# Second attention of a four-layer block: two maxima blocks and the second half of the query transposes move into the next step, the split terms get a second buffer

## The reference, cut to what matters

```python
hn = _layernorm(x, ln1_g, ln1_b)                    # 16 sequences of 256 tokens, 16 heads of width 8
q = (hn @ wq + bq); k = (hn @ wk + bk); v = (hn @ wv + bv)
scores = jnp.einsum('bhqd,bhkd->bhqk', q, k) / jnp.sqrt(jnp.float32(D))
attn = jax.nn.softmax(scores, axis=-1)
o = jnp.einsum('bhqk,bhkd->bhqd', attn, v)
x = x + (o @ wo + bo)
hn2 = _layernorm(x, ln2_g, ln2_b).reshape(-1, h)
logits = hn2 @ gate_w + gate_b
idx = jnp.argmax(logits, axis=-1)                   # one expert for each token
```

## Time and profile before

| | us |
|---|---|
| median of 3 runs | 1882.75 (1875.11 to 1886.69) |
| the profiled execution | 1882.32 |
| its span | 1880.5 |
| PE, DVE, POOL, ACT busy in the span | 1255.7, 1244.0, 1018.8, 727.4 |
| granted PE clock, mean of the span | 0.761 |

### The profile page before, as it was taken

How to read it: one execution, slowest core, us unless ns; L and a number is a source line. 1 busy time by engine, 2 the same in 40 slices (tenths; PEclk the granted TensorE clock), 3 DMA queues, 4 the chain that set the end, 5 groups by cost and what they waited for, 6 DMA issues and landing times.

```text
span 1880.5 us, 28307 instructions
## 1 busy us (share of the span) xinstructions
PE 1255.7 (67%) x8634; PEld 880.8 (47%) x8635; DVE 1244.0 (66%) x2728; ACT 727.4 (39%) x1190; POOL 1018.8 (54%) x1176
## 2 busy tenths in 40 slices
PE   3435333478777777877787779257767776746796
PEld 1223122236666565656665558223433333325685
DVE  6788850177787878787878873167777778743322
ACT  1101001145454454454444553036565555532221
POOL 2356576456666666666666645334445444425554
PEclk7555555578888888888888887669898889878766
DMA  4010004400000000000000000210000000001110
GB/s 132 22 27 15 13 13 81 94 7 1 8 8 8 7 6 6 6 6 6 6 3 3 7 4 6 72 33 12 19 18 16 9 17 17 7 17 44 42 40 12
DMA packets 73354, 40.91 MB, mean 22 GB/s; under 512 B 23811, under 2 KB 68716, under 8 KB 73284
## 3 DMA queue, kind: packets, MB, share of 16 engines
q1 hardware_dynamic: 50530, 24.02, 4.6%
q0 software_dynamic: 20384, 11.67, 3.1%
q10 hardware_dynamic: 2370, 4.35, 0.8%
HBM read 31.11 MB, written 23.87 MB: 29 GB/s over the span
## 4 chain that ended last, share of the span: by engine, by line
PE 33%; DVE 29%; issue 13%; POOL 13%; ACT 7%; DMA 2%; ACTq 1%; POOLq 1%; SPq 0%; DVEq 0%; another core or an unknown queue 0%
PE psum L1138 9%; PE psum L1189 5%; POOL xe_dram L570 4%; DVE terms L1766 4%; DVE o L1606 4%; PE psum L1246 3%; POOL o_inv L618 3%; DVE q_highT L1792 2%; PE psum L1166 2%; POOL got L768 2%; POOL out L777 2%; PE psum L1304 1%; DVE rden L1458 1%; PE psum L1269 1%; DVE silu_g L1700 1%
## 5 line engine op out<-in xcount | busy, mean ns | idle before, releaser
L1138 PE MATMUL psum<-v,attn 128*128 128x64 f32 x2048 | 287.8, 300 | 25.6 <-ACT aggr L870 17.1
L1138 PEld LDWEIGHTS psum<-v,attn 128*128 128x128 f32 x2048 | 271.9, 213 | 61.1 <-issue 44.2
L1766 DVE TENSOR_REDUCE terms<-psum 128x4 bf16<-128x1024 f32 x128 | 156.9, 1226 | 45.5 <-PE psum L1269 43.7
L641 POOL DMA_INDIRECT yg<-ye_dram,routel x128 | 140.1, 1095 | 60.0 <-issue 36.2
L945 ACT ACTIVATE prob<-psum 128x512 f32<-128x512 f32 x256 | 139.5, 602 | 49.7 <-PE psum L1233 45.5
L570 POOL DMA_INDIRECT xe_dram<-rows_out,route x128 | 131.8, 1030 | 39.6 <-issue 39.0
L855 ACT ACTIVATE attn<-psum 128x1024 f32<-128x1024 f32 x128 | 129.9, 1015 | 10.1 <-PE psum L1121 8.9
L1147 PE MATMUL psum<-ident,o 128*128 128x128 f32 x256 | 48.7, 353 | 117.9 <-DVE silu_g L1700 91.0
L618 POOL TENSOR_TENSOR o_inv<-o_max,minus_half 128x16 f32<-128x16 f32 x32 | 107.6, 3364 | 2.7
L658 POOL TENSOR_TENSOR v<-v,inv 128x2048 f32<-128x2048 f32 x16 | 70.7, 4418 | 59.8 <-DVE inv L1586 59.8
L1147 PEld LDWEIGHTS psum<-ident,o 128*128 128x128 f32 x256 | 39.1, 183 | 131.5 <-DVE o L1606 66.5
(11 more groups left out here) (300 smaller groups left out, 3106.5 us busy)
## 6 DMA issues: line engine op xcount, KB each, us to landing
x4n_dram<-x4n SPq DMA_DIRECT2D x16, 256.0 KB, 4.5
w<-in_w POOLq DMA_DIRECT2D x48, 64.0 KB, 2.3
x_in<-in_x SPq DMA_DIRECT2D x8, 256.0 KB, 2.9
xe_dram<-zero_rows SPq DMA_DIRECT2D x8, 256.0 KB, 3.2
x_dram<-x1s SPq DMA_DIRECT2D x8, 256.0 KB, 2.4
xe_dram<-rows_out,route POOLq DMA_INDIRECT x128, 2.1
xe<-xe_dram SPq DMA_DIRECT2D x16, 128.0 KB, 2.4
ye_dram<-ye SPq DMA_DIRECT2D x16, 128.0 KB, 2.2
```

The lines of the kernel that those rows point to most:

```text
L641: pool.indirect_dma_start(yg[fetch.p][:, j, k, :], None, ye_dram, bass.IndirectOffsetOnAxis(ap=where[:, j, K0 + k:K0 + k + 1], axis=0), bo ...
L1138: mm = pe.matmul(psum[:, 4 + j, (head % HALF) * DV:(head % HALF + 1) * DV], attn[g % RING][:, h, c * SEQ + j * P:c * SEQ + (j + 1) * P], v ...
L1766: dve.tensor_reduce(dst[:, :, 2 * m2:2 * m2 + 2], psum[:, 4:6, :].rearrange("q p (b k) -> q p b k", b=2), AX, ALU.max, negate=True).then_i ...
```

## The change

`terms4` becomes two buffers, one for odd and one for even sequences; POOL clears both before the first step, and POOL, ACT and DVE may overwrite one as soon as the sequence two before has been transposed. Maxima blocks 6 and 7 leave part 7 and are done in parts 0 and 1 of the next step, as work of `att`, on PE ahead of that part's scores. Blocks 0 to 5 take parts 3, 4, 5, 6, 7, 7. q4 half 1 goes from part 1 to part 3, q4 half 0 from part 6 to part 7, behind the transposes of `xn4`, which now come ahead of those of `x4n`. The transposes of `o4` use ring[0] where they used ring[1], and ACT copies them out in part 4 behind two more exponentials. On DVE the expert choice comes directly behind the logits, and the residual add with its moments comes ahead of block 1. On POOL the roots of the first normalisation come ahead of the sum that it adds up for the end of the tail.

```diff
-        terms4 = sb("terms4", [P, 2, 2, HEADS, TERMS1, DH], BF16)
+        terms4 = two("terms4", [P, 2, 2, HEADS, TERMS1, DH], BF16)
...
-            pool.memset(terms4[:], 0.0).then_inc(s["set4"], 1)
             for p in range(2):
+                pool.memset(terms4[p][:], 0.0).then_inc(s["set4"], 1)
                 pool.memset(v4[p][:], 0.0).then_inc(s["set4"], 1)
...
             for p in range(2):
+                pool.memset(terms4[p][:, 1, :, :, MAXIMUM, 0:1].rearrange("q j h a -> q (j h) a"), 1.0).then_inc(s["set4"], 1)
                 pool.memset(v4[p][:, :, :, DH:DH + 1], 1.0).then_inc(s["set4"], 1)
...
-                    if not isinstance(front.n, int) or front.n > 1:
-                        hold(s["q4_ps"], 2 * (front.n - 1))
+                    if not isinstance(front.n, int) or front.n > 2:
+                        hold(s["q4_ps"], 2 * (front.n - 2))
...
                 if tail:
                     inverse_deviation("var5", meanvar5, veps5, rstd5, "rstd5", tail.n)
+                if fetch:
...
+                    inverse_deviation("var4", meanvar4, veps4, rstd4_in, "rstd4_in", fetch.n)
...
+                if tail:
                     if not isinstance(tail.k, int) or tail.k > 1:
                         hold(s["x4_stored"][tail.p], 16 * (tail.k - 1))
                     hold(s["plain_made"], tail.n)
                     pool.tensor_tensor(x4n[tail.p][:, :, 0:D], x4[tail.p][:], x3_plain[tail.p][:], ALU.add).then_inc(s["sum_made"], 1)
                 if fetch:
...
-                    if att and g == 1:
+                    if att and g == 3:
                         take_terms(att, "q4", 1, 1)
...
-                    if tail and g == 3:
+                    if tail and g == 4:
                         act.wait_ge(s["o4T_ps"], tail.n)
-                        act.activation(o4T[:], ring[1][:, 0:SEQ], ACT.Copy).then_inc(s["o4T_made"], 1)
+                        act.activation(o4T[:], ring[0][:, 0:SEQ], ACT.Copy).then_inc(s["o4T_made"], 1)
...
-                    if front and g == 6:
+                    if fetch and g == 7:
+                        act.wait_ge(s["x4T_ps"], fetch.n)
+                        act.activation(h4T[:], ring[1][:, 0:SEQ], ACT.Identity, bias=norms[:, 1:2], scale=norms[:, 0:1]).then_inc(s["h4T_made"], 1)
+                    if front and g == 7:
                         take_terms(front, "q4", 0, 1)
                     if tail and g == 7:
                         act.wait_ge(s["x5T_ps"], tail.n)
                         act.activation(h5T[:], ring[0][:, 0:SEQ], ACT.Identity, bias=norms[:, 3:4], scale=norms[:, 2:3]).then_inc(s["h5T_made"], 1)
-                    if fetch and g == 7:
...
-                if front:
+                if att:
+                    readers[1] = [(s["q4_out"], 2 * att.n - 1)]
+                elif front:
                     readers[1] = [(s["h4T_made"], front.n)]
-                elif att:
-                    readers[1] = [(s["q4_out"], 2 * att.n - 1)]
                 elif end:
                     readers[1] = [(s["x4_made"], end.n)]
                 for g in range(PAIRS):
+                    if att and g < 2:
+                        maxima(att, 6 + g)
                     if att:
                         scores4(att, g)
                     if tail and g == 0:
@@ -1302,8 +1306,6 @@
...
-                    if att and g == 1:
-                        turn_terms(att, "q4", 1, 1, [(s["max_made"], PAIRS * att.n), (s["terms4_made"], 6 * att.n)])
                     if end and g == 1:
...
+                    if att and g == 3:
+                        turn_terms(att, "q4", 1, 1, [(s["max_made"], PAIRS * att.n), (s["terms4_made"], 6 * att.n)])
                     if front and g in (3, 4, 5, 6, 7):
-                        maxima(front, (0, 1, 3, 4, 6)[g - 3])
+                        maxima(front, g - 3)
...
                     if tail and g == 3:
-                        b = fill4(1, [(s["o4T_made"], tail.n)], [(s["o4_made"], 2 * tail.n)])
+                        b = fill4(0, [(s["o4T_made"], tail.n)], [(s["o4_made"], 2 * tail.n)])
...
-                    if front and g == 6:
-                        turn_terms(front, "q4", 0, 1, [(s["max_made"], PAIRS * (front.n - 1) + 4), (s["terms4_made"], 6 * front.n)])
                     if att and g == 6:
                         turn_values(att, 0, 0)
+                    if fetch and g == 7:
+                        b = fill4(1, [(s["h4T_made"], fetch.n)], [(s["xn4_made"], fetch.n)])
+                        for j in range(2):
+                            mm = pe.transpose(b[:, j * P:(j + 1) * P], xn4[:, j, :], ident[:])
+                        mm.then_inc(s["x4T_ps"], 1)
+                    if front and g == 7:
+                        turn_terms(front, "q4", 0, 1, [(s["max_made"], PAIRS * (front.n - 1) + 4), (s["terms4_made"], 6 * front.n)])
                     if tail and g == 7:
                         b = fill4(0, [(s["h5T_made"], tail.n)], [(s["x4n_made"], tail.n)])
                         for j in range(2):
                             mm = pe.transpose(b[:, j * P:(j + 1) * P], x4n[tail.p][:, j, D:2 * D], ident[:])
                         mm.then_inc(s["x5T_ps"], 1)
-                    if fetch and g == 7:
-                        b = fill4(1, [], [(s["xn4_made"], fetch.n)])
-                        for j in range(2):
-                            mm = pe.transpose(b[:, j * P:(j + 1) * P], xn4[:, j, :], ident[:])
-                        mm.then_inc(s["x4T_ps"], 1)
-                    if front and g in (4, 6, 7):
-                        maxima(front, {4: 2, 6: 5, 7: 7}[g])
+                    if front and g == 7:
+                        maxima(front, 5)
...
             def half(fetch, front, att, tail, end):
                 for g in range(PAIRS):
+                    if att and g < 2:
+                        take_maxima(att, 6 + g)
                     if front and g == 0:
...
-                    if end and g == 2:
+                    if end and g == 1:
                         for j in range(2):
...
-                    if front and g in (3, 4, 5, 6):
-                        take_maxima(front, (0, 1, 3, 4)[g - 3])
+                    if front and g == 1:
+                        dve.wait_ge(s["high4_made"], front.n)
+                        dve.tensor_tensor(qk4[:], qk4[:], high4[:], ALU.subtract).then_inc(s["rest4_made"], 1)
...
+                    if tail and g == 2:
+                        divide_by_sums(tail, 1, 1)
+                    if front and g == 3:
+                        wait(dve, s["q4_ps"], 2 * (front.n - 2))
+                        take_maxima(front, 0)
                     if end and g == 3:
...
-                    if front and g == 4:
-                        take_maxima(front, 2)
+                    if front and g in (4, 5):
+                        take_maxima(front, g - 3)
                     if fetch and g == 5:
...
                     if front and g == 6:
-                        take_maxima(front, 5)
+                        take_maxima(front, 3)
                     if fetch and g == 7:
...
                     if front and g == 7:
-                        take_maxima(front, 6)
-                        take_maxima(front, 7)
+                        take_maxima(front, 4)
```

More of the change, by code:

```diff
@@ L730, in half @@
                     inverse_deviation("var5", meanvar5, veps5, rstd5, "rstd5", tail.n)
-                    if not isinstance(tail.k, int) or tail.k > 1:
-                        hold(s["x4_stored"][tail.p], 16 * (tail.k - 1))
-                    hold(s["plain_made"], tail.n)
-                    pool.tensor_tensor(x4n[tail.p][:, :, 0:D], x4[tail.p][:], x3_plain[tail.p][:], ALU.add).then_inc(s["sum_made"], 1)
                 if fetch:
@@ L748, in half @@
                     pool.tensor_tensor(rstd4[:], rstd4_norm[:], rstd4_in[:], ALU.mult).then_inc(s["rstd4"], 1)
+                if tail:
+                    if not isinstance(tail.k, int) or tail.k > 1:
+                        hold(s["x4_stored"][tail.p], 16 * (tail.k - 1))
+                    hold(s["plain_made"], tail.n)
+                    pool.tensor_tensor(x4n[tail.p][:, :, 0:D], x4[tail.p][:], x3_plain[tail.p][:], ALU.add).then_inc(s["sum_made"], 1)
+                if fetch:
                     chain.step(pool.tensor_scalar(x3n[fetch.p][:, 0, :], x3l[fetch.p][:, 0, :], meanvar4[:, 0, 0:1], rstd4_in[:, 0:1], ALU.subtract, ALU.mult))
@@ L986, in half @@
                         act.activation(h5T[:], ring[0][:, 0:SEQ], ACT.Identity, bias=norms[:, 3:4], scale=norms[:, 2:3]).then_inc(s["h5T_made"], 1)
-                    if fetch and g == 7:
-                        act.wait_ge(s["x4T_ps"], fetch.n)
-                        act.activation(h4T[:], ring[1][:, 0:SEQ], ACT.Identity, bias=norms[:, 1:2], scale=norms[:, 0:1]).then_inc(s["h4T_made"], 1)
             pipeline(act, half, 5)
@@ L1278, in turn_terms @@
                         at = (2 * a4 + j) * P
```

(2 more changed lines are left out.)

39 lines of the change are left out of this document (17 added, 22 removed).

## The result

| | before | after |
|---|---|---|
| median | 1883.11 us (4 runs, 1875.11 to 1886.69) | 2081.06 us (4 runs, 2063.16 to 2087.19) |
| ratio | | 1.104, 95% interval 1.097 to 1.111 |
| profiled execution's span | 1880.5 | 2061.2 |
| a step, mean of steps 5 to 14 | 26.99 | 39.72 |
| granted clock of PE in these steps | 0.87 | 0.65 |

The change costs 198 us; the forecast said 96, and 2081 lies over its range. The profiled execution is the fastest of the four (2063.16, granted clock 0.718 over the span; the others 0.703 to 0.707 at 2081 to 2087).

A forecast was written before the change was run, and what follows sets the result against it. No engine fills a step; in-order engines wait for each other in one closed chain of sections A, B, C. 82 us for 12 steps, 11 for others, 3.5 for a memset: 96 on 1882.3 gives 1978 us, range 1918 to 2010.

The forecast's parts named there:

- The clock of PE: PE's granted clock in the changed stage: the sum leaves it at 0.87 although a step grows to 33.8 us.
- the sum: A, B and C together: 6.8 us a full step, 82 for 12 steps; with other steps and memset 96 us.
- a rival with 11 in 100: Second rival: PE's clock falls from 0.87 to 0.72, 2.2 us more a step, 2004 us; 11 in 100.
- A: Step's border, from `xn4`'s end to DVE's first bias add: grows 3.2 us, qkv behind two maxima rounds on PE.
- B: From first bias add to block 0's reduce end: grows 1.3 us, mostly block 0 waiting behind q4 half 1.
- C: From block 0's reduce to `xn4`'s end: grows 2.3 us despite two rounds fewer, as y4 and block 1 come late.
- The bank of `picked_b`: In C: `o4` transposes wait for ring[0], read by `picked_b` after block 0's reduce; they start 0.17 us after that reduce.
- Other steps: Steps 1, 2, 3, 16 and 17, counted alike: together +11 us, of which step 3 +5.9.
- The first rival: Moved blocks fill DVE's idle time and ring waits do not bind: -2.2 us a step, 1856 us; 6 in 100.
- the third: A grows as worked out, but `o4T` is early enough that C keeps its two rounds: 1883 us; 9 in 100.
- the fourth: A binds, q4 half 1 finds its bank free, late y4 just eats the two rounds: 1932 us; 17 in 100.

The follow-up runs named there:

- w2: Changed kernel plus 32 PE products a step that nothing reads, ahead of eight PE waits, 12 of them ahead of q4 half 1: 1981.6 us.
- c1: Changed kernel with block 1's reduce ahead of the residual add on DVE again, no added products: 2028.9 us.
- w4: w2 without the 12 added products ahead of q4 half 1, those at the seven other waits kept: 1990.6 us.
- wch: w2 with DVE's expert choice put back behind the division of part 2: 1949.7 us.
- wc: w2 with block 1's reduce ahead of the residual add on DVE: 1962.3 us.
- wbco: wb with block 1 ahead of the residual add, `o4` transposes ahead of the rank products, ACT's copy a part earlier, no added products ahead of y4: 1949.9 us.
- wbest: wch with block 5 directly behind the transposes of `xn4`, block 1 ahead of the residual add, no added products ahead of block 6: 1927.3 us.
- w3: Kernel before the change plus 16 PE products a step that nothing reads, ahead of six PE waits: 1871.6 us, ratio 0.996.
- wb: w2 with q4 half 1 behind block 0, values 0 and the rank products, and 6 added products there instead of 12: 1964.8 us.
- wfull: wbco with block 5 directly behind the transposes of `xn4` and no added products ahead of block 6: 1930.0 us.
- w1: Changed kernel plus three larger products a step that nothing reads, in PE's long pause ahead of q4 half 1: 2057.1 us.
- b1: Changed kernel with q4 half 1 behind block 0, values and rank products on PE, no added products: 2046.8 us.

## Why the prediction was wrong, step by step

**The step that failed** is the one under "The clock of PE": "The changed step leaves PE the same work in 33.8 us", and still the sum kept 0.87. The fall was made a rival with 11 in 100, to 0.72, at 1.5 us for a tenth from two steps, 26 us in all; against it stood "that PE still gets the same bursts". Measured: the same bursts, with longer pauses between them, got 0.65, and from after to w2 39.72 - 33.73 = 6.0 us for 0.28, 2.1 for a tenth (added work in the way would make it look smaller; c1's steps of two lengths give 3.5), 99 us in the whole time. The price was a poor reading too: in the same trace of before, 1567.80:1594.80 takes 27.00 us at 0.94 and 1485.70:1513.80 takes 28.10 at 0.89. In the new order more PE work is on the chain: at the border q4 half 0, the transposes of `x4n` and two blocks stand between the transposes of `xn` and qkv, where one block stood; whether that is why the price is higher was not tested. And waits and clock feed each other, which a fixed fall leaves out: the longer waits of the new order came with a lower clock, and when w2 gave the clock back, DVE's waits for PE shrank with no change to the order (in ten steps, for the maxima blocks from 71.5 us to 46.9, for qkv from 28.6 to 9.7; for y4 hardly, 31.3 to 30.3). What the Trainium skill says (TensorE: Matmul & The Clock Gate, "What's actually happening"), that activity releases the low clock, the runs bear out: added work that nothing reads took 99 us off.

**The order's own cost** was sized nearly right: at w4's 0.88 a step is 34.33, so 7.3 us more than before where the sum had 6.8. That w2 comes within 4 us of 1978 is partly luck: its clock is not the 0.87 of the sum, and B came out 1.5 longer, C 0.8 shorter.

**A** (+3.2): right at the restored clock, 7.45 for 7.21; first in order are the transposes, then two rounds, then qkv, as laid out. In after itself, at half clock, 10.95.

**B** (+1.3): too small, 12.29 for 10.8 in w2. Three places carry the 1.5: block 0's wait (1.80 for 1.18), the comparison that makes the one-hot rows (0.73 for 0.17) and the eight masks (2.81 for 2.48). "The expert choice moves within B and costs nothing" is wrong: put back, it takes 1.85 off B and 2.7 off a step (w2 to wch: 33.73 to 31.04), the clock's part in it included. I costed the new wait of q4 half 1 (1.18; 1.80 in w2) without seeing that the choice had stood where it would have covered it, nor that the rank products would now end behind block 0's reduce (0.75).

**C** (+2.3): right in its mechanism, 14.06 for 14.9 in w2. y4 is late (wait 2.53), block 1 behind it; up to the division it is 1606.27 - 1594.44 = 11.83 for 11.93, and only the rest is shorter, by `xn4`'s two instructions (0.60 us for 1.31). wc shows block 1's place as 19 us, a rise of the clock to 0.96 included. The bank of `picked_b` does hold up the transposes of `o4`, by 0.27 us a step in w2; that it is the main cause of the late y4 is not shown, since wbco, which takes `o4` out from behind it, made a wait of its own.

**Other steps.** Step 3 grew by 12.8 us for 5.9, steps 4 to 15 by 151.6 for 82, both with the clock.

**What would show it.** DVE's waits for y4, block 0 and block 5 and PE's for the division (5.18) came as said; block 6 waits 0.81, not over 1. The step, 37 to 41 us where 32 to 35 was said, and DVE's share, 54.5% for 63%, were the signs against the clock. The first rival falls on the first add, 10.95 us behind `xn4`, the third on the wait for y4, the fourth on PE's wait of 5.18 us for the bank that it took to be free.

**What stays open.** wbest undoes the choice, block 1 and block 5's place and is still 2.7 us a step over w3 (29.1 to 26.4). By the two chains A has 2.6 of it and B 1.0, while C, in which DVE waits 2.4 a step for the division, is not longer. So q4 half 0 and block 6 ahead of qkv, and block 7 in B, are the candidates; with the choice back in its place they were not tried.

## What to carry to other kernels

Where PE has half-idle steps, a forecast that lengthens a step has to price PE's work on the chain at the clock that the longer step will have, and go round once more; the sum at the old clock was only half of the loss here. Before an instruction is moved because its engine has time elsewhere, look at what it covers where it stands: DVE's choice covered PE's q4 half 1. To find an order's own price, fill PE's pauses with work that nobody reads, and compare there; but look whether PE still waits behind that work. Where it did not (wb, wbco, wfull), the added work was a delay of its own.

## What was not expected of the hardware

The long pause is not what lowers the clock most: 0.70 with most of the 5.2 us filled, 0.88 with the seven others filled (w1, w4), and 0.65 with real work in its place (b1). A tuned kernel gains 0.4% from work that nobody reads. DVE's one-hot comparison, two operands in SBUF, took 0.73 us in w2, where POOL's copy runs beside it, and 0.17 in wch, where none does; the eight masks took 2.48 us in the kernel before, 2.81 in w2 and 3.53 in wch, and POOL is busy for 1.60, 2.02 and 3.05 us of these times; whether POOL is the reason was not tried. The Trainium skill (SBUF — State Buffer, "Who interferes with whom") has a DVE instruction with two SBUF inputs contend with one of GpSimd that reads SBUF; the one-hot's two durations agree. POOL in w2:

```profile
1585.87 0.83 POOL L715 COPY terms<-high 128x768 bf16<-128x768 bf16 x1
```
